# Ternary feed-forward up projection: one fp32 product against three summed float32r products

## What is computed

```python
def _bitlinear(x, w_latent):
    scale = clip(mean(abs(w_latent), axis=1, keepdims=True), 1e-05, None)
    tern = clip(round(w_latent / scale), -1.0, 1.0)
    w = w_latent + (tern - w_latent)
    return x @ (w * scale).T
h = _bitlinear(x, w_fc) + gate * (x @ v.T @ fast_b.T @ u.T)
r = maximum(h, 0.0)
return _bitlinear(r * r, w_proj)
...
x = x + _L1_ffn_ref(_layernorm(x, axis=-1), ...)
```

## Time and profile before

| | us |
|---|---|
| three runs | 3518.75, 3519.7, 3526.47 |
| median | 3519.7 |
| span of the profiled execution, first to last instruction | 3506.0 |
| ternary stage in that span | about 3352 to 3503 |
| TensorE busy, share of the span | 3144.6, 90% |
| VectorE, ScalarE, GpSimd busy | 70%, 65%, 44% |
| mean granted TensorE clock | 0.947 of full |

### The profile page before, as it was taken

One profiled execution on the slowest core, in us unless ns is written; L12 is line 12 of the kernel. 1 busy time (PEld: TensorE's weight loads), 2 busy tenths in 40 slices (PEclk: granted clock), 3 DMA queues, 4 the chain that ended last, 5 costly groups with the idle time before them and its releaser, 6 DMA issues. The chain is left out here.

```text
span 3506.0 us, 72683 instructions
## 1 busy us (share of the span) xinstructions
PE 3144.6 (90%) x22614; PEld 1680.9 (48%) x22614; DVE 2452.0 (70%) x6945; ACT 2276.8 (65%) x3088; POOL 1534.6 (44%) x1807
## 2 busy tenths in 40 slices
PE   6999995898988884987299999999999999999978
PEld 2555552454544452554144444444444444444456
DVE  4666655888777752332678888888888888888754
ACT  4777771555555562222678888888888888888723
POOL 3444442345455523565634333444333444433443
PEclk9999995899999996999599999999999999999989
DMA  4444443222222212443300000000000000000001
GB/s 100 119 118 103 108 100 84 55 61 64 66 53 54 64 40 66 126 142 101 106 7 0 9 0 9 0 9 0 3 6 2 7 0 9 0 9 0 0 16 34
DMA packets 173142, 162.16 MB, mean 46 GB/s; under 512 B 18276, under 2 KB 156735, under 8 KB 172830
## 3 DMA queue, kind: packets, MB, share of 16 engines
q1 hardware_dynamic: 163838, 142.35, 16.7%
q0 software_dynamic: 9088, 16.88, 1.4%
HBM read 92.40 MB, written 68.52 MB: 46 GB/s over the span
## 5 line engine op out<-in xcount | busy, mean ns | idle before, releaser
L546 ACT ACTIVATE ga_PT<-ga_S 128x1024 f32<-128x1024 f32 (+1 forms) x384 | 336.3, 880 | 286.2 <-PE ga_S L373 283.0
L2717 POOL TENSOR_TENSOR lb_y<-lb_ao,XC 128x512 f32<-128x512 f32 x128 | 163.2, 1275 | 807.3 <-ACT lb_ao L2664 807.3
L2556 PE MATMUL lb_H<-lb_x,lb_w 128*128 (+1 forms) x1024 | 513.8, 604 | 0.5 <-issue 0.5
L2565 PE MATMUL lb_FF<-lb_h,lb_w 128*128 128x512 f32 x1024 | 460.3, 592 | 0.0
L2671 ACT ACTIVATE lb_h<-lb_H,lb_prm 128x512 f32<-128x512 f32 x512 | 351.7, 687 | 99.8 <-PE lb_H L2556 84.7
L2763 DVE TENSOR_SCALAR lb_z<-lb_M,lb_mv,lb_rstd 128x128 f32<-128x128 f32 x1024 | 349.9, 404 | 32.8 <-POOL lb_rstd L2708 9.4
L2565 PEld LDWEIGHTS lb_FF<-lb_h,lb_w 128*128 128x128 f32 x1024 | 194.6, 190 | 244.9 <-issue 215.4
L2708 POOL TENSOR_TENSOR lb_rstd<-lb_rstd,half 128x4 f32<-128x4 f32 x256 | 259.5, 1014 | 37.0 <-issue 0.2
L2755 DVE BATCH_NORM_STATS2 lb_stats<-lb_M 128x6 f32<-128x128 f32 x1024 | 228.3, 285 | 30.9 <-PE lb_M L2538 23.0
L2556 PEld LDWEIGHTS lb_H<-lb_x,lb_w 128*128 128x128 f32 x1024 | 174.0, 190 | 132.3 <-issue 122.8
L1521 POOL TENSOR_SCALAR_AFFINE_SELECT da_PT<-da_PT 128x1024 f32<-128x1024 f32 x128 | 146.1, 1146 | 196.3 <-ACT da_PT L1451 196.3
(11 more groups left out here) (330 smaller groups left out, 7087.7 us busy)
## 6 DMA issues: line engine op xcount, KB each, us to landing
moe_w<-experts_dram SPq DMA_DIRECT2D x39, 384.0 KB
da_qT<-da_stq SPq DMA_DIRECT2D x64, 192.0 KB, 4.3
da_kT<-da_stk SPq DMA_DIRECT2D x64, 192.0 KB, 5.2
ga_qT<-ga_stq SPq DMA_DIRECT2D x32, 384.0 KB, 6.0
moe_x<-moe_xs SPq DMA_DIRECT2D x39, 258.0 KB
tc_g<-moe_ys SPq DMA_DIRECT2D x32, 256.0 KB, 3.2
da_stq<-da_parts SPq DMA_DIRECT2D x16, 384.0 KB, 2.4
da_stk<-da_parts SPq DMA_DIRECT2D x16, 384.0 KB, 3.1
```

Of the source, the lines that this page charges most:

```text
L546: act.activation(PT[:, n % RING, :, lo:hi], score_banks(u)[:, :, 0:hi - lo], ACT.Exp, scale=SCALE).then_inc(probs, 1)
L2556: pe.matmul(H[:, k % 2, :], w1[:, k, :], x1_of(i), start=True, stop=True).then_inc(h_filled, 1)
L2565: pe.matmul(FF[:, :], w2[:, k, :], h[:, k, :], start=(k == 0), stop=(k == KC - 1)).then_inc(ff_filled, 1)
L2717: pool.tensor_tensor(y1[:, :], ao[:, :], state(i), ALU.add).then_inc(y1_ready, 1)
```

## The change

`wfcT` gets a second half, and both halves have the type float32r. The first takes ScalarE's copy of the weights (the high part, as float32r keeps it), the second what VectorE subtracts: the weights minus the high part. The same is done to xT in every iteration: ScalarE's copy gives the high part, and a new VectorE step `rest_of_x` gives M minus the high part. `up` then sums three products per chunk: high weights x high x, rest weights x high x, high weights x rest x. The product rest x rest is left out. The low part of x has a semaphore of its own, on which the third product of the first chunk waits, and `turn` now waits for it instead of for the copy, since `rest_of_x` reads M too.

```diff
     W = {...
-         "wfcT": sb("wfcT", [P, 4, P]), "wprT": sb("wprT", [P, 4, P])}
+         "wfcT": sb("wfcT", [P, 2, 4, P], F32R), "wprT": sb("wprT", [P, 4, P])}
...
-        xT = sb("xT", [P, 2, SEQ])
+        xT = sb("xT", [P, 2, 2, SEQ], F32R)
...
             def turn(c):
                 pe.wait_ge(xn_ready, c + 1)
                 if c:
-                    pe.wait_ge(xT_copied, c)
+                    pe.wait_ge(xT_low_ready, c)
...
             def up(b):
-                pe.wait_ge(xT_copied, b + 1)
+                s = b % 2
+                pe.wait_ge(xT_high_ready, b + 1)
                 for k in range(KC):
                     if b:
                         pe.wait_ge(relu_ready, KC * (b - 1) + k + 1)
-                    pe.matmul(HB[:, k, :], wfcT[:, k, :], xT[:, b % 2, :], start=True, stop=True
+                    for part in range(2):
+                        pe.matmul(HB[:, k, :], wfcT[:, part, k, :], xT[:, s, 0, :],
+                                  start=(part == 0), stop=False)
+                    if k == 0:
+                        pe.wait_ge(xT_low_ready, b + 1)
+                    pe.matmul(HB[:, k, :], wfcT[:, 0, k, :], xT[:, s, 1, :], start=False, stop=True
                               ).then_inc(h_filled, 1)
...
-                act.activation(xT[:, c % 2, :], M[:, :], ACT.Copy).then_inc(xT_copied, 1)
+                act.activation(xT[:, c % 2, 0, :], M[:, :], ACT.Copy).then_inc(xT_high_ready, 1)
...
+            def rest_of_x(c):
+                v.wait_ge(xT_high_ready, c + 1)
+                v.tensor_tensor(xT[:, c % 2, 1, :], M[:, :], xT[:, c % 2, 0, :].bitcast(F32),
+                                ALU.subtract).then_inc(xT_low_ready, 1)
...
             add_back(1)
             measure(1)
             centre(1)
+            rest_of_x(0)
             for b in range(NB):
                 for k in BY_DVE:
...
+                if b + 1 < NB:
+                    rest_of_x(b + 1)
                 if b + 2 < NB:
                     add_back(b + 2)
                     measure(b + 2)
...
                 if k == 3:
                     act.wait_ge(wfcT_filled, 1)
-                    act.activation(W["wfcT"][:, :, :], Q[:, :].rearrange("p (k n) -> p k n", k=KC),
-                                   ACT.Copy)
+                    act.activation(W["wfcT"][:, 0, :, :], Q[:, :].rearrange("p (k n) -> p k n", k=KC),
+                                   ACT.Copy).then_inc(wfcT_high_ready, 1)
...
+                if k == 4:
+                    v.wait_ge(wfcT_high_ready, 1)
+                    v.tensor_tensor(W["wfcT"][:, 1, :, :],
+                                    Q[:, :].rearrange("p (k n) -> p k n", k=KC),
+                                    W["wfcT"][:, 0, :, :].bitcast(F32), ALU.subtract)
```

More of the change, by code:

```diff
@@ L7 @@
 BF16 = mybir.dt.bfloat16
+F32R = mybir.dt.float32r
 ALU = mybir.AluOpType
@@ L2113, in ternary_weights, with sb @@
 def ternary_weights(nc, C, ctx):
-    def sb(name, shape):
-        return ctx.enter_context(nc.sbuf_tensor("ff_" + name, shape, F32))
+    def sb(name, shape, dt=F32):
+        return ctx.enter_context(nc.sbuf_tensor("ff_" + name, shape, dt))
     W = {"wfc": sb("wfc", [P, 4, P]), "wpr": sb("wpr", [P, 512]), "uT": sb("uT", [16, 512]),
@@ L2172, in ternary_stage @@
         xT_filled = sem("xT_filled")
-        xT_copied = sem("xT_copied")
+        xT_high_ready = sem("xT_high_ready")
+        xT_low_ready = sem("xT_low_ready")
         h_filled = sem("h_filled")
@@ L2452, in linear_blocks @@
         wprT_filled = sem("wprT_filled")
+        wfcT_high_ready = sem("wfcT_high_ready")
         W, tern_loaded = C["ff_weights"], C["ff_loaded"]
```

## The result

The changed kernel takes **3539.1 us** (median of 4 runs, 3536.8 to 3543.1) against 3522.2 for the kernel before (4 runs beside them, 3518.8 to 3526.5): 16.9 us more, ratio 1.0048 with a 95% interval of 1.0034 to 1.0062. It is slower, as forecast (3536.5 from a base of 3519.7, +16.8).

The account below looks back on a forecast made before the run. TensorE was taken as the bound, with one 0.80 us hole hanging on VectorE's order. Start +5.1, chain +5.4, clock +8.9 and last three iterations -2.6 gave +16.8 on 3519.7: 3536.5 us, range 3525.0 to 3549.

Parts of the forecast that it names:

- start, to `up(2)`: First iterations: `up(0)` waits for the low part and `add_back(2)` and `add_back(3)` come later; +5.1 us, bounds 2.5 to 7.
- chain, 11 periods: Steady part: copy, subtraction and `add_back` take 1.35 us, products give 0.86; period 9.39 instead of 8.90, +5.4 us.
- clock: Steady part: a 3.24 us gap without products makes the granted clock fall in half of eleven periods, 1.62 each; +8.9 us.
- last three iterations: End of the stage, without `back`: TensorE waits for nobody, so the cheaper products give 3 x 0.86; -2.6 us.
- The mechanism: VectorE's queue: the subtraction stands ahead of `add_back`, which TensorE's `back` waits for; that wait grows from 0.80 to about 2.1 us.
- The product: `up` on TensorE: a float32r product costs 0.215 us, three replace one fp32 product of 0.86; 0.86 us less per `up`.
- The first half: Start, to `add_back(2)`: a TensorE idle of 2.6 us inside `up(0)`, other ten passes at half clock; +4.15 us.
- The second half: Start, from `add_back(2)` to `add_back(3)`, which follows `turn(2)` by 2.03 instead of 1.07 us; +0.96 us.
- The tail: The last three iterations, without `back`: TensorE waits for nobody and gains 3 x 0.86; -2.6 us.
- The weights' remainder: Preparation: one more VectorE instruction of 0.69 us after `ternary(3)`, covered by 1.3 us until ScalarE ends; 0.
- The span and the median: Profiled span of 3506.0 us is 13.7 less than the median 3519.7; what lies around the span does not change.
- The weight loads: `up` on TensorE: 128 added loads of 190 ns fit under the products; exposed, they would cost 2.3 us an iteration.

Follow-up runs that it names:

- e1_add_back_first: Changed kernel with `rest_of_x(b+1)` moved behind `add_back(b+2)` and `measure(b+2)` in VectorE's loop; 3520.4 us, ratio 0.9989 to the kernel before.
- e3_chain_before: Kernel before, fp32 products kept, with VectorE's subtraction alone added into a scratch tile that `turn` waits for; 3540.7 us, ratio 1.0050 to the kernel before.
- e4_fill_gap: Changed kernel with six more float32r products per iteration between `turn` and `back`, from b = 1 on; 3530.1 us, ratio 1.0019 to the kernel before.
- e6: Changed kernel with three more 128-column products at the head of each `down`; stage 170.9 us in one execution, where the changed kernel took 167.1.
- e9: Changed kernel with the second and third product of each chunk over 256 columns instead of 512; stage 167.3 us in one execution.
- e5: Kernel before with the subtraction chain added and three of the sixteen products of `down` left out (output incomplete); stage 163.8 us in one execution.

## Why the prediction was right, step by step

| term | forecast | measured |
|---|---|---|
| start, to `up(2)` | +5.1 | +2.2 |
| chain, 11 periods | 11 x 0.49 = +5.4 | 11 x 0.62 = +6.8 |
| clock | 5.5 x 1.62 = +8.9 | 5 x 1.62 = +8.1 |
| last three iterations | -2.6 | -1.1 |
| sum | +16.8 | +16.0 (stage), +16.9 (medians) |

**The mechanism** holds: e1_add_back_first removes it and e3_chain_before reproduces it without the products. What `back` waits for is the copy, the subtraction and `add_back` in a row.

**The product** was mis-sized. The rows had it: 0.457 ns a column from the bf16 rows is 0.234 us for 512. I wrote 0.23 and then took half an fp32 record, 0.215. The gain per `up` was 0.56 us and not 0.86.

**The chain** was a little cheaper than I put it, 1.18 instead of 1.35 on the same offsets (the subtraction took 0.61 from start to start instead of 0.70, and `back` to the next `up` 3.98 instead of 4.06), so the missing 0.30 us of gain an `up` came down to 0.13 a period. An fp32 product measures as 3.7 float32r products (0.86 against 0.234); the forecast's four was this ratio rounded. That float32r runs at the cheap end of the bounds, which no row had shown, is now shown.

**The clock** was right in size and number, by a guess at the number. The falls cost 1.62 each in the changed kernel and in e4_fill_gap by their absence. That half the gaps would be caught was an estimate between 0 and 11; e3, e6 and e9 show 0, 1 and 10 for other periods, and e5 5 again for nearly the same one, so the estimate was right for this period only, and that is luck. The rule from the Trainium skill's "TensorE: Matmul & The Clock Gate", section "Part 4: PE-mode transpose", that transposes do not count as busy in the same way, agrees: the gap of 3.15 us holds eight transposes and only 2.06 us of idle time, and the clock fell. No run here tells transposes from idle time, since the products of e4_fill_gap took the place of idle time.

**The start** was too dear by 2.9 us. The first half was nearly right, `up(0)` to `up(1)` 10.60 us instead of 7.31 (+3.3, forecast +4.15): the hole inside `up(0)` was 2.17 us, not 2.6, and the clock rose at 3385.5, ahead of its last products, where I had all ten passes at half clock. The second half had the wrong sign: `up(1)` to `up(2)` took 10.72 instead of 11.78. I had kept the cold `down(0)` of the kernel before, and in the changed one the fall came earlier, at 3388.9, over `up(1)`, and was over at 3392.3. `down(0)` ran warm.

**The tail** was too cheap by 1.5: 3 x 0.56 is 1.7, and `turn(15)` came 0.65 late. I had written that of the steps behind the subtraction only `add_back` has someone waiting, and that failed here: `centre(15)` waits for the `rstd` that GpSimd makes from `measure`, and `turn(15)` waits for `centre(15)`:

```profile
3521.65 1.92 DVE L2304 TENSOR_SCALAR ff_xn<-XT,ff_mv,ff_rstd 128x128 f32<-128x128 f32 x4 [0.59 <-POOL ff_rstd L2268]
...
3523.62 0.66 PE L2198 MATMUL ff_M<-ident,ff_xn 128*128 128x128 f32 x4 [0.50 <-DVE ff_xn L2304]
```

Without `back`, TensorE doesn't wait, reaches the next `up` sooner, and then this later link of the same VectorE queue comes last.

**The weights' remainder** cost nothing, as forecast: at 3369.06 for 0.68 us, while ScalarE ended the linear blocks at 3371.14.

**The span and the median.** I put the 13.7 us between the profiled span and the median down to what lies around the span. In the changed kernel span and time of one execution differ by 1.8 us (3541.3 and 3543.05), so most of the 13.7 was a difference between executions. It didn't enter the sum. The weight loads, which I had given 2.3 us an iteration if exposed, are covered.

**The total** is closer than its terms. Start and clock were too dear by 2.9 and 0.8, chain and tail too cheap by 1.4 and 1.5, and in the sum this leaves 0.8. The direction and the mechanism were foreseen; that the total came within 1 us is luck.

## What to carry to other kernels

When work moves from the engine that is the bound to another one, ask where in that engine's queue it stands. Here 0.7 us of subtraction stood ahead of the one step that TensorE waits for, and cost more than the cheaper products gave. The same instruction two places later took the loss away, and with the start's order mended as well the change is a gain of 0.24%. A wait that grows on TensorE can cost twice: in this stage, where it brought the time without products to some 3 us, the clock fell in some periods and not in others, and a shorter period had more falls. So a stage's time is not a smooth function of its work. Read such stages on the trace, and count the falls and their cost apart from the chain.

## What the runs showed of the hardware

- A float32r product of 128x128 weights follows the one before by 0.457 ns a column (0.234 us for 512, 0.117 for 256) at full clock, the slope of the bf16 durations; an fp32 product of 512 columns takes 0.86 us. The weight load of 0.19 us in front of each product doesn't show in the distance, not even at 0.117 (e9_half_columns).
- A granted clock of 0.50 lasted 3.4 us at each fall of the steady parts, and a fall within 1 us of the start of a `down` cost 1.62 us (1.54 in e6_long_down).
- With the same gap of 3.15 us between real products the clock fell 5, 5, 0 and 1 times in eleven periods of 9.52, 9.49, 10.17 and 10.20 us; at a period of 8.71 and a gap of 3.16 us (3368.38 to 3371.54) it fell ten times. At a gap of 2.31 us (e1_add_back_first) or 1.89 us (before) it didn't fall in the steady part. These are counts of one execution each.
- VectorE's second square took 1.04 us where it had taken 0.77, once the relus came 0.70 us apart and GpSimd's squares lay beside 0.79 us of it instead of 0.22. What slows it wasn't tried apart. It wasn't on the path here, since the copy ended later; in e1_add_back_first it is, and what it costs there wasn't tried either.
